# A transformer front with its rotation, mask, norms and tile loop arranged anew

## The reference

```python
h = rmsnorm(hidden, ln1_w)                  # hidden = layernorm(x), resid = hidden
q = rope(h @ Wq, pos)                       # 32 heads of 128
k = rope(h @ Wk, pos)                       # 4 key heads of 128, each for 8 query heads
v = h @ Wv
scores = q @ k.T / sqrt(128), causal        # 56 x 56 for each sample and head
resid = hidden + softmax(scores) @ v @ Wo
t = rmsnorm(resid, ln2_w)
s = sigmoid(t @ Wr)                         # 32 experts
idx = top_k(s + expert_bias, 8)
w = s[idx] / sum(s[idx])                    # goes on to the experts, with t

def rope(x, pos):                           # halves of the 128 columns of a head
    x1, x2 = split(x, 2)
    return concat([x1*cos - x2*sin, x1*sin + x2*cos])
```

## Time and profile before

| | us |
|---|---|
| three runs | 4922.49, 4909.76, 4930.6; median 4922.49 |
| the profiled execution | 4918.62 |
| its span (first to last instruction) | 4916.8 |
| busy in the span: PE, DVE, ACT, POOL | 4145.4, 2627.2, 2014.4, 1614.0 |
| first copy of the changed stage to its last output projection | 577.4 |
| its fill, tile 0, 1, 2, 3 in the first pass | 46.5, 56.5, 64.1, 60.7, 56.1 |

### The profile page before, as it was taken

How to read it: one execution, slowest core, us unless ns; L and a number is a source line. 1 busy time by engine, 2 the same in 40 slices (tenths; PEclk the granted TensorE clock), 3 DMA queues, 4 the chain that set the end, 5 groups by cost and what they waited for, 6 DMA issues and landing times. The chain is left out here.

```text
span 4916.8 us, 79350 instructions
## 1 busy us (share of the span) xinstructions
PE 4145.4 (84%) x30154; PEld 3401.5 (69%) x30154; DVE 2627.2 (53%) x5937; ACT 2014.4 (41%) x3336; POOL 1614.0 (33%) x1130
## 2 busy tenths in 40 slices
PE   6999449996868799699999965669999999999967
PEld 5777338885756544377777753359999999999963
DVE  5777554446757411266666662545555555555542
ACT  5777323332212211156555542234444444444421
POOL 3333013332212122111111101446556556556521
PEclk9999659997988899889998988779999999999988
DMA  3333025530000122111111111321001101001002
GB/s 117 99 102 101 26 70 171 162 88 1 1 1 1 58 78 90 38 49 46 47 37 50 43 52 37 85 69 30 30 27 30 31 26 31 30 26 30 27 1 68
DMA packets 168182, 259.20 MB, mean 53 GB/s; under 512 B 75916, under 2 KB 141644, under 8 KB 159036
## 3 DMA queue, kind: packets, MB, share of 16 engines
q1 hardware_dynamic: 167820, 254.25, 17.3%
HBM read 236.25 MB, written 17.98 MB: 52 GB/s over the span
## 5 line engine op out<-in xcount | busy, mean ns | idle before, releaser
L694 DVE CUSTOM_DVE_ANT_0 xh_soft<-xh_s,xh_mask 128x500 f32<-128x500 f32 x768 | 491.1, 675 | 150.6 <-PE xh_s L606 145.8
L616 PEld LDWEIGHTS xh_t<-tables,xh_soft 128*125 128x125 f32 x3072 | 383.0, 197 | 67.2 <-issue 46.1
L858 ACT ACTIVATE xh_probsT<-xh_t 125x512 f32<-125x512 f32 x640 | 339.6, 598 | 219.1 <-PE xh_t L616 218.9
L616 PE MATMUL xh_t<-tables,xh_soft 128*125 128x128 f32 x3072 | 417.8, 291 | 4.9 <-ACT xh_probsT L858 4.2
L851 ACT ACTIVATE xh_soft<-xh_soft,xh_neg_max 128x1500 f32<-128x1500 f32 x256 | 392.6, 1545 | 17.4 <-DVE xh_neg_max L702 17.4
L1312 DVE CUSTOM_DVE_ANT_0 xg_soft<-xg_s,xgw_mask 128x500 f32<-128x500 f32 x384 | 246.6, 677 | 283.3 <-PE xg_s L1222 282.4
L878 POOL TENSOR_TENSOR xh_ctx_low<-xh_ctxT,xh_ctx_high 128x1000 fp32r<-128x1000 f32 x96 | 223.5, 2346 | 519.8 <-ACT xh_ctx_high L838 516.2
L1411 POOL TENSOR_TENSOR xg_soft<-xg_soft,xg_recip 128x1500 f32<-128x1500 f32 x128 | 344.0, 2687 | 10.0
L1366 ACT ACTIVATE xg_soft<-xg_soft,xg_neg_max 128x1500 f32<-128x1500 f32 x128 | 198.1, 1548 | 332.8 <-DVE xg_neg_max L1316 332.8
L1246 PE MATMUL xg_o<-xg_probsT,xg_values 125*128 125x224 f32 x1536 | 303.0, 354 | 6.2 <-ACT xg_probsT L1373 5.3
L1246 PEld LDWEIGHTS xg_o<-xg_probsT,xg_values 125*128 125x128 f32 x1536 | 287.2, 191 | 7.2 <-ACT xg_probsT L1373 5.6
(11 more groups left out here) (483 smaller groups left out, 10625.0 us busy)
## 6 DMA issues: line engine op xcount, KB each, us to landing
xh_ctxT<-ctxT SPq DMA_DIRECT2D x32, 1500.0 KB, 7.4
xh_values<-ctx SPq DMA_DIRECT2D x16, 1500.0 KB
x_ctxT<-ctxT SPq DMA_DIRECT2D x16, 1500.0 KB, 22.2
x_ctx_rows<-ctx SPq DMA_DIRECT2D x16, 1500.0 KB
xgw_raw<-ctxT SPq DMA_DIRECT2D x48, 500.0 KB, 4.0
f1b_weight<-f_weights SPq DMA_DIRECT2D x32, 448.0 KB, 4.5
xh_mask<-mask_BxSxS_ff SPq DMA_DIRECT2D x32, 328.1 KB
f1b_wgu<-f_wgu SPq DMA_DIRECT2D x33, 256.0 KB, 2.8
```

The costliest lines, as they stand in the source:

```text
L616: mm = pe.transpose(bank[0:KC, i * 128:(i + 1) * 128], soft[m % 8][:, n * KC:(n + 1) * KC], ident)
L694: v.tensor_tensor_reduce(soft[m % 8][:, j * THIRD:(j + 1) * THIRD], bank[:, 0:THIRD], add, 1.0, -3.0e38, ALU.add, ALU.max, tops[g % 2][:, ...
L858: a.activation(probsT[m % 4][:, 4 * q:4 * q + 4, :], bank[0:KC, :].rearrange("p (i n) -> p i n", i=4), ACT.Copy).then_inc(copied, 1)
```

## The change

- `TILES = 8`: all tiles in one pass. The plan is twice as long, and the loop goes round once.
- The rotation: ACT no longer copies the group's bank as it is but in two halves of 64 partitions, each to the other's place (`swapped`). VectorE multiplies the bank itself by the cosines and `swapped` by the sines, all 128 partitions at once, and adds. POOL has no part in it. The bank is released by VectorE after the first multiply. The table of sines has the sign in the other half.
- The mask: scale and add in one instruction; the separate pass that added -1e9 is gone.
- The norms: P becomes P, P2, P3, P4, and H0's norm becomes H2 and H3, each one VectorE instruction or a few, with rotations between them. The router's two steps are now called H4 and H5.

```diff
-    c[:, C_SIN:C_SIN + SLOT] = np.concatenate([np.sin(ang), -np.sin(ang)], 1).T
+    c[:, C_SIN:C_SIN + SLOT] = np.concatenate([-np.sin(ang), np.sin(ang)], 1).T
...
-    plan = [("P", 0, 0), ("PT", 0, 0), ("V", 0, 0)] + [("R", 0, i) for i in range(5)] + [("P", 1, 0)]
-    plan += [("R", 0, i) for i in range(5, 9)] + [("PT", 1, 0)]
+    def norm(u):
+        return [(op, u, 0) for op in ("P", "P2", "P3", "P4")]
+
+    plan = norm(0) + [("PT", 0, 0), ("V", 0, 0)] + [("R", 0, i) for i in range(2)]
+    for op in norm(1):
+        plan += [op, ("R", 0, len([key for key in plan if key[0] == "R"]))]
+    plan += [("R", 0, i) for i in range(6, 9)] + [("PT", 1, 0)]
     for u in range(tiles):
         ahead = [("V", u + 1, 0)] + [("R", u + 1, i) for i in range(9)] if u + 1 < tiles else []
         behind = [("A", u - 1, i) for i in range(4)] if u else []
-        late = [(h, u - 1, 0) for h in ("H0", "H1", "H2", "H3")] if u else []
+        late = {n: [(op, u - 1, 0)] for n, op in ((0, "H2"), (1, "H3"), (2, "H1"), (4, "H4"), (7, "H5"))} if u else {}
+        early = dict(zip(range(5), [[op] for op in norm(u + 2)] + [[("PT", u + 2, 0)]])) if u + 2 < tiles else {}
         for i in range(4):
 
             some = AHEAD[u > 0][i]
             plan += [("S", u, i)] + ahead[:some] + behind[:1] + [("N", u, i - 1)] * (i > 0)
             ahead, behind = ahead[some:], behind[1:]
         some = AHEAD[u > 0][4]
-        plan += late[:1] + ahead[:some] + [("N", u, 3)]
-        ahead, late = ahead[some:], late[1:]
+        plan += [("H0", u - 1, 0)] * (u > 0) + ahead[:some] + [("N", u, 3)]
+        ahead = ahead[some:]
         for n in range(8):
             some = 2 if len(ahead) > 8 - n else 1
             plan += [("T", u, n)] + ahead[:some] + [("O", u, n - 1)] * (n > 0)
             ahead = ahead[some:]
-            if n in LATE:
-                plan, late = plan + late[:1], late[1:]
-            if n == P_AT and u + 2 < tiles:
-                plan += [("P", u + 2, 0)]
-            if n == PT_AT and u + 2 < tiles:
-                plan += [("PT", u + 2, 0)]
-        plan += [("O", u, 7)] + late
-    return plan + [("A", tiles - 1, i) for i in range(4)] + [(h, tiles - 1, 0) for h in ("H0", "H1", "H2", "H3")]
+            plan += late.get(n, []) + early.get(n - 1, [])
+        plan += [("O", u, 7)]
+    u = tiles - 1
+    return plan + [("A", u, i) for i in range(4)] + [(op, u, 0) for op in ("H0", "H2", "H3", "H1", "H4", "H5")]
...
-    NH, KV, HD, TILES = 32, 4, 128, 4
+    NH, KV, HD, TILES = 32, 4, 128, 8
...
-                    def rmsnorm(src, key):
+                    def mean_square(key):
+                        v.wait_ge(s["squared"], norms[key] + 1)
+                        v.tensor_scalar(ms[:, :], ms[:, :], 1.0 / D, 1e-5, ALU.mult, ALU.add).then_inc(s["ms_ready"], 1)
+
+                    def scaled_row(src, key):
                         i = norms[key]
-                        v.wait_ge(s["squared"], i + 1)
-                        v.tensor_scalar(ms[:, :], ms[:, :], 1.0 / D, 1e-5, ALU.mult, ALU.add).then_inc(s["ms_ready"], 1)
                         v.wait_ge(s["h_rstd"], i + 1)
                         if i:
                             before = [k for k in norms if norms[k] == i - 1][0]
...
                     def turn(u, i):
                         r = GROUPS * u + i
-                        sb.copied(v, ("rope", u, i))
-                        src, turned = raw[i % 2 ^ u % 2], by_sin[i % 2 ^ u % 2]
+                        bank, copied = sb.get(v, ("rope", u, i))
+                        v.wait_ge(s["swapped"], 2 * r + 2)
+                        src = swapped[r % 2]
                         if r:
                             v.wait_ge(s["rope"], r)
...
-                        v.tensor_tensor(by_cos[:, :, :, :].rearrange("p h b q -> p (h b) q"), src[:, :, :, :].rearrange(
-                            "p h b q -> p (h b) q"), again(cos, 8), ALU.mult).then_inc(s["cos_done"], 1)
-                        v.tensor_tensor(turned[0:64, :, :, :].rearrange("p h b q -> p (h b) q"), src[64:128, :, :, :].rearrange(
-                            "p h b q -> p (h b) q"), again(sin[64:128, :], 8), ALU.mult).then_inc(s["turned_v"], 1)
+                        v.tensor_tensor(by_cos[:, :, :, :].rearrange("p h b q -> p (h b) q"), bank[:, :].rearrange(
+                            "p (a q) -> p a q", a=8), again(cos, 8), ALU.mult).then_inc(s["cos_done"], 1)
+                        v.tensor_tensor(by_sin[:, :, :, :].rearrange("p h b q -> p (h b) q"), src[:, :, :, :].rearrange(
+                            "p h b q -> p (h b) q"), again(sin, 8), ALU.mult).then_inc(s["turned"], 1)
                         v.wait_ge(s["cos_done"], r + 1)
-                        v.wait_ge(s["turned_v"], r + 1)
-                        v.wait_ge(s["turned_p"], r + 1)
+                        v.sem_inc(copied, 1)
+                        v.wait_ge(s["turned"], r + 1)
                         dst = keysT[u % 2][:, :, :, :] if i == 0 else \
                             queriesT[u % 2][:, :, 4 * (i - 1):4 * i, :].rearrange("p b h q -> p h b q")
-                        v.tensor_tensor(dst, by_cos[:, :, :, :], turned[:, :, :, :], ALU.add).then_inc(s["rope"], 1)
+                        v.tensor_tensor(dst, by_cos[:, :, :, :], by_sin[:, :, :, :], ALU.add).then_inc(s["rope"], 1)
...
-                                               in1=again(c[:, C_KEEP0:C_KEEP0 + SQ], 8), op0=ALU.mult,
-                                               op1=ALU.mult).then_inc(copied, 1)
+                                               in1=again(c[:, C_ADD1:C_ADD1 + SQ], 8), op0=ALU.mult,
+                                               op1=ALU.add).then_inc(copied, 1)
                         sb.copied(v, ("s", u, n))
-                        v.tensor_tensor(work[:, :, :], work[:, :, :], again(c[:, C_ADD1:C_ADD1 + SQ], 8), ALU.add).then_inc(s["v"], 1)
-                        v.wait_ge(s["v"], step())
...
                         if op == "P":
-                            layernorm_vector(v, s, step, ln, tile_of(core.x, t * TILES + u), u)
+                            if u:
+                                v.wait_ge(s["h_ready"], norms["P", u - 1] + 1)
+                            layernorm_start(v, s, step, ln, core.x[:, u, :])
+                        elif op == "P2":
+                            layernorm_end(v, s, ln, u)
                             v.wait_ge(s["xn_ready"], u + 1)
-                            v.tensor_copy(normed[u % 3][:, :], ln.xn[:, :]).then_inc(s["v"], 1)
-                            v.wait_ge(s["v"], step())
-                            rmsnorm(ln.xn, (op, u))
+                            v.tensor_copy(normed[u % 3][:, :], ln.xn[:, :]).then_inc(s["normed"], 1)
+                        elif op in ("P3", "H2"):
+                            mean_square(("P" if op == "P3" else "H0", u))
+                        elif op == "P4":
+                            scaled_row(ln.xn, ("P", u))
+                        elif op == "H3":
+                            scaled_row(x2, ("H0", u))
...
                         elif op == "R":
-                            bank, copied = sb.get(a, ("rope", u, n))
+                            bank, _ = sb.get(a, ("rope", u, n))
                             r = GROUPS * u + n
                             if r >= 2:
-                                a.wait_ge(s["rope"], r - 1)
-                            a.activation(raw[n % 2 ^ u % 2][:, :, :, :].rearrange("p h b q -> p (h b q)"), bank[:, :],
-                                         ACT.Copy).then_inc(copied, 1)
+                                a.wait_ge(s["turned"], r - 1)
+                            for to, at in ((slice(0, 64), slice(64, 128)), (slice(64, 128), slice(0, 64))):
+                                a.activation(swapped[r % 2][to, :, :, :].rearrange("p h b q -> p (h b q)"), bank[at, :],
+                                             ACT.Copy).then_inc(s["swapped"], 1)
...
-                        if op in ("P", "H0"):
-                            g.wait_ge(s["ms_ready"], norms[op, u] + 1)
-                            if norms[op, u]:
-                                g.wait_ge(s["h_ready"], norms[op, u])
+                        elif op in ("P3", "H2"):
+                            i = norms["P" if op == "P3" else "H0", u]
+                            g.wait_ge(s["ms_ready"], i + 1)
+                            if i:
+                                g.wait_ge(s["h_ready"], i)
                             g.tensor_tensor(rstd[:, :], ms[:, :], core.minus_half[:, 0:1], ALU.pow).then_inc(s["h_rstd"], 1)
-                            g.wait_ge(s["h_rstd"], norms[op, u] + 1)
-                        elif op == "R":
-                            r, j = GROUPS * u + n, n % 2 ^ u % 2
-                            sb.copied(g, ("rope", u, n))
-                            if r >= 2:
-                                g.wait_ge(s["rope"], r - 1)
```

(23 more changed lines are left out.)

10 lines of the change are left out of this document (4 added, 6 removed).

## The result

The changed kernel takes 4799.9 us (median of four runs, 4794.0 to 4802.3) where the kernel before takes 4916.1 (4904.8 to 4930.6): a ratio of 0.976, 95% interval 0.973 to 0.979. The forecast was 4838 with a range from 4806: right in sign, too small in size, and outside the range. The profiled execution took 4794.0 us, its span is 4791.8.

The account below looks back on a forecast made before the run. VectorE's rotations bound the second half of each front-stage tile, and PE's stops cost extra. Fill 38.7, tile 0 48.5, tiles 1 to 5 300, tile 6 55.5, tile 7 54.6: 497.3 against 577.4, so 4838 us (4806 to 4870).

Follow-up runs that it names:

- the joining alone: The kernel before with one pass over eight tiles in place of two over four, and nothing else: 4869.5 us, ratio 0.992.

## What to carry to other kernels

When a change shortens a stop of PE, don't subtract its terms from the tile's length alone: compare PE's busy time for the same matmuls in a tile with the stop and in one without, and take the difference out with the stop. And price every edit against the engine that will bound afterwards: a saving measured alone (9.1 us for the norms) can be next to nothing (1.4) beside another that makes it idle time. Where PE is within a few us of being the bound, two places in the order of the work (a row ahead of the router, a group one step earlier) were here worth 19 us of 463.

## What was not expected of the hardware

- What a stop of PE costs beyond its length grows with it in the mean, and varies between equal stops: behind 1.57 us nothing in 21 cases of 32 and 1.7 or 3.3 us of PE time in the others, behind 2.3 us nothing, 1.7 or 3.3, behind 3.0 us 1.7 or 3.3, behind 4.5 us 3.3 in all six, and about 4.3 more in the full tiles of the joining alone, with stops of 6.
- An elementwise product of 128x512 on VectorE lets the next one start after 0.61 us when both are on all 128 partitions, from PSUM or from SBUF, and after 0.72 when the next is on 64 partitions and reads the other 64 (1189.32 to 1190.04 in the kernel before).
